# Causal attention of four heads in one query tile, values by query tile, and narrower rank comparisons, in an eight-stage graph model

## What is computed

```python
# x = x + _L1_ffn_ref(_layernorm(x), ...)
weights = (jnp.einsum('bsd,do->bso', x, wr) + br)[..., 0]
_, idx = jax.lax.top_k(weights, k)
sel_idx = idx[:, :kk]
h = jax.nn.gelu(jnp.einsum('bkd,dh->bkh', sel, w1) + b1)
y = jnp.einsum('bkh,hd->bkd', h, w2) + b2
y = y * w_sel[..., None]
processed = jnp.zeros_like(x).at[batch_idx, sel_idx].set(y)
return processed + x
...
# inside x = x + _L3_ffn_ref(x, ...)
q = q * cos + _rotate_half(q) * sin
k = k * cos + _rotate_half(k) * sin
scores = jnp.einsum('bhtd,bhsd->bhts', q, k) / jnp.sqrt(jnp.float32(HD))
scores = jnp.where(causal[None, None], scores, jnp.float32(-1e+30))
att = jax.nn.softmax(scores, axis=-1)
y = jnp.einsum('bhts,bhsd->bhtd', att, v).transpose(0, 2, 1, 3).reshape(Bx, Tx, Cx)
x = x + y @ wo.T
```

## Time and profile before

| | |
|---|---|
| median of 3 runs | 4642.03 us (4640.98 to 4642.9) |
| the profiled execution, by the same clock as the runs | 4647.35 us |
| its span, first to last instruction | 4645.3 us |
| mean granted clock of PE in it | 0.824 |
| busy in the span: PE, DVE, ACT, POOL | 76%, 61%, 44%, 37% |
| the mod stage | about 2465 to 2666 us of the span |
| the mha3 stage | about 3628 to 4212 us of the span |

### The profile page before, as it was taken

The page is one execution under the profiler, slowest core; times in us unless marked ns, Lnnn a source line. Parts: engine busy times, 40 slices in busy tenths (PEclk is TensorE's granted clock), DMA queues, the critical chain, the costliest instruction groups (busy, mean ns, idle before and its releaser), DMA issues. The chain is left out here.

```text
span 4645.3 us, 80348 instructions
## 1 busy us (share of the span) xinstructions
PE 3532.3 (76%) x23571; PEld 2150.4 (46%) x23571; DVE 2839.6 (61%) x10823; ACT 2067.0 (44%) x5218; POOL 1717.0 (37%) x2167
## 2 busy tenths in 40 slices
PE   3999995666666649999896776479847788874994
PEld 1333334444444423333364566357636555542663
DVE  5677756555555566777588967612277566653444
ACT  1777773322222217777632265334347444441221
POOL 3555520000000014343293137744446444344445
PEclk9999995555555559999998987689969998986997
DMA  4444429500000024433100022144342000002445
GB/s 128 125 135 130 126 63 390 231 0 0 0 0 0 0 80 124 122 110 115 50 0 2 9 86 73 48 132 145 118 144 83 1 10 16 14 19 75 130 130 164
DMA packets 235811, 386.80 MB, mean 83 GB/s; under 512 B 25344, under 2 KB 157568, under 8 KB 227136
## 3 DMA queue, kind: packets, MB, share of 16 engines
q1 hardware_dynamic: 217152, 345.83, 22.8%
q0 software_dynamic: 18432, 38.31, 2.4%
HBM read 210.70 MB, written 173.34 MB: 83 GB/s over the span
## 5 line engine op out<-in xcount | busy, mean ns | idle before, releaser
L1482 DVE CUSTOM_DVE_ANT_0 mha_seen<-mha_score,mha_mask 128x512 f32<-128x512 f32 x1024 | 682.7, 688 | 378.6 <-PE mha_score L1245 372.5
L1386 ACT ACTIVATE mha_prob<-mha_turned 128x512 f32<-128x512 f32 x1024 | 587.3, 602 | 305.8 <-PE mha_turned L1259 298.1
L1638 PE MATMUL lstm_gates<-lstm_h_part,lstm_w_part 128*128 128x16 f16 x4608 | 278.8, 179 | 327.9 <-DVE lstm_h_part L1853 324.5
L1245 PE MATMUL mha_score<-mha_k_rows,mha_q_rows 96*128 96x512 bf16 x1024 | 398.7, 391 | 59.4 <-DMA mha_k_rows<-split_rows 39.0
L3152 POOL DMA_INDIRECT expert_rows<-expert_y,expert_target x320 | 306.5, 958 | 367.6 <-DVE expert_y L3298 150.8
L1638 PEld LDWEIGHTS lstm_gates<-lstm_h_part,lstm_w_part 128*128 128x128 f16 x4608 | 217.2, 107 | 481.2 <-DVE lstm_h_part L1853 475.5
L1259 PE MATMUL mha_turned<-mha_q_rows,mha_k_rows 99*128 99x512 bf16 x1024 | 390.0, 382 | 7.9 <-ACT mha_turned L1370 6.4
L1585 POOL TENSOR_TENSOR core_mid<-lstm_hist,lstm_per_unit 128x128 f32 x64 | 29.3, 458 | 888.0 <-DVE lstm_hist L1854 888.0
L1725 ACT ACTIVATE lstm_act<-lstm_gates 128x48 f32<-128x48 f32 x512 | 107.5, 210 | 429.7 <-PE lstm_gates L1638 429.7
L1258 PE MATMUL mha_turned<-mha_maskT,core_ident_bf 128*128 128x512 bf16 x768 | 295.0, 384 | 0.5 <-ACT mha_prob L1386 0.3
L3190 PEld LDWEIGHTS expert_out_ps<-expert_w,expert_hid 128*128 128x128 f32 (+1 forms) x2240 | 262.4, 191 | 39.3 <-issue 37.1
(11 more groups left out here) (550 smaller groups left out, 8834.7 us busy)
## 6 DMA issues: line engine op xcount, KB each, us to landing
routed_rows<-lstm_blank SPq DMA_DIRECT2D x66, 1056.0 KB, 26.9
gat_adj_raw<-adj SPq DMA_DIRECT2D x32, 1024.0 KB, 5.5
mha_q_rows<-split_rows SPq DMA_DIRECT2D x64, 384.0 KB, 4.0
mha_k_rows<-split_rows SPq DMA_DIRECT2D x64, 384.0 KB, 4.9
expert_x<-routed_rows SPq DMA_DIRECT2D x80, 264.0 KB
expert_w<-weights SPq DMA_DIRECT2D x80, 256.0 KB
core_params<-adj SPq DMA_DIRECT2D x16, 1024.0 KB, 6.1
combine_pair<-expert_rows SPq DMA_DIRECT2D x32, 512.0 KB, 4.9
```

The source lines that it names most:

```text
L1245: pe.matmul(score[n % 2][:, :], rows[0][s][0:ROWS, h, t * P:(t + 1) * P], rows[1][s][0:ROWS, h, :], start=True, stop=True).then_inc(S["sco ...
L1386: act.activation(prob[:, n % RING, :], turned[n % 3][:, :], ACT.Exp, scale=-1.0).then_inc(S["prob_ready"], 1)
L1482: dve.tensor_tensor_reduce(seen[n % 2][:, :], score[n % 2][:, :], mask[1 - s][:, t, :], 1.0, 3e38, ALU.add, ALU.min, low[g][:, t, j:j + 1] ...
L1638: return pe.matmul(out, w[:, g * P:(g + 1) * P], h_part[:, part, :], start=False, stop=stop, skip_group_check=True)
```

## The change

In mod: the comparisons of tile t cover only the columns in which their mask isn't zero, 0 to (t+1)·128 and t·128 to 512; the bias `mb2` is cut into three bf16 parts at the stage's start (`cut_bias`, DVE) and added by a bf16 matmul of ones with 512 columns ahead of `out`; POOL adds `xn` and the old rows (`residual`, to `base`), and DVE's last step multiplies, adds and writes the rows at once.

In mha3: one query tile per graph with all heads; scores read rows 32j to 32j+31 of it and of `kT`; the value products are made per query tile, each once its four items are copied; projections go one to an item; POOL sends rows before it makes the scales; the memsets of the query tiles and the wait `landed` are gone.

```diff
-            at = {"rows": 0, "early": (2, 4), "values": 3, "back": 6, "ctx": 9, "out": 11, "v": 12}
+            at = {"rows": 0, "early": (2, 3, 4, 5), "values": 3, "back": 7, "ctx": 10, "out": 12, "v": 13}
...
-                    if first:
-                        pool.wait_ge(S["zeros_set"], 8)
                     if b >= 4:
                         pool.wait_ge(S["r_scaled"], (b - 2) // 2)
-                    if b >= 6:
-                        router.landed(pool, (b - 6) // 2, b % 2)
-                    for j in range(4):
-                        rows = slice(32 * j, 32 * j + 32)
-                        pool.tensor_tensor(qT[s][j][rows, :], part[rows, 0, :], part[rows, 1, :], ALU.add)\
-                            .then_inc(S["rot_ready"], 1)
-                    pool.wait_ge(S["rot_ready"], 5 * b + 4 + 5)
+                    pool.tensor_tensor(qT[s][:, :], part[:, 0, :], part[:, 1, :], ALU.add).then_inc(S["rot_ready"], 1)
...
                     graph(b, b % 2, first=b == 0)
                 if b + 1 < B:
                     normalise(b + 1)
+                if b >= 5:
+                    half = (b - 5) % 2 * T
+                    router.scatter(pool, (b - 5) // 2, range(half, half + T))
                 if b % 2 and 0 <= (b - 3) // 2 < B // 2:
                     pool.wait_ge(S["tail"], (b - 1) * (2 * T + 3))
                     router.scales(pool, (b - 3) // 2)
-                if b >= 5:
-                    half = (b - 5) % 2 * T
-                    router.scatter(pool, (b - 5) // 2, range(half, half + T))
 
...
             def scores(b, s, n):
                 g, t, j = n // (4 * T), tile_of(n), n % 4
                 if n == 0 and rope:
-                    pe.wait_ge(S["rot_ready"], 5 * b + 5 + 5)
+                    pe.wait_ge(S["rot_ready"], 2 * b + 2 + 2)
                 elif n % (4 * T) == 0:
                     pe.wait_ge(S["qk_ready"], projections * b + 2 * g + 2 + 1)
                 pe.wait_ge(S["score_taken"], items * b + n + 1)
                 width = keys(t) * P
                 pair = s if rope else g
-                pe.matmul(score[n % 2][:, 0:width], qT[pair][j][:, t * P:(t + 1) * P], kT[pair][:, 0:width], start=True, stop=True)\
+                own = slice(32 * j, 32 * j + 32)
+                pe.matmul(score[n % 2][:, 0:width], qT[pair][own, t * P:(t + 1) * P], kT[pair][own, 0:width], start=True, stop=True)\
                     .then_inc(S["score_done"], 1)
...
-            def values(b, g, s):
-                done = b * (items // 2) + 2 * T * (g + 1) + 1
-                if g == 0:
+            def values(b, k, s):
+
+                t = ORDER[k]
+                own = slice(t * P, (t + 1) * P)
+                done = b * (items // 2) + 2 * (k + 1) + 1
+                if k == 0:
                     pe.wait_ge(S["v_ready"], b + 1 + 1)
-                pe.wait_ge(S["oT_ready"], groups * b + g + 1)
+                    pe.wait_ge(S["oT_ready"], b + 1)
                 pe.wait_ge(S["probT_act"], done)
                 pe.wait_ge(S["probT_dve"], done)
-                for u in range(T):
+                for u in range(keys(t)):
                     for j in range(4):
-                        first = u * P if rope else 0
-                        last = pe.matmul(o_ps[g][32 * j:32 * j + 32, first:], v32[s][:, u, 4 * g + j, :], probT[:, j, u, first:],
-                                         start=(u == 0), stop=(u == T - 1))
+                        last = pe.matmul(o_ps[0][32 * j:32 * j + 32, own], v32[s][:, u, j, :], probT[:, j, u, own],
+                                         start=(u == 0), stop=(u == t))
...
-                        values(b - 1, groups - 1, 1 - s)
-                    if n == at["values"] + 4 * T:
-                        values(b, 0, s)
+                        values(b - 1, T - 1, 1 - s)
+                    if n > 4 and n % 4 == at["values"]:
+                        values(b, n // 4 - 1, s)
...
             def copy_probT(b, n):
                 act.wait_ge(S["prob_free"], items * b + n + 1 + PR)
-                if n % (4 * T) == 0:
-                    act.wait_ge(S["pv_done"], groups * b + n // (4 * T) + 1)
+                if n % 4 == 0 and b:
+                    act.wait_ge(S["pv_done"], T * (b - 1) + n // 4 + 1 + 1)
...
-            rows_.normalise_all(pool)
+            pool.memset(bias_ones[:, :], 1.0).then_inc(S["bias_set"], 1)
...
+            def residual(b, s):
+
+                pool.wait_ge(S["xn_ready"], b + 1)
+                if not isinstance(b, int) or b >= 2:
+                    pool.wait_ge(S["x_taken"], b - 1)
+                apart(pool, core)
+                pool.tensor_tensor(base[s][:, :, :], rows_.xn[b % 3][:, :, :], core.x_res[:, b], ALU.add).then_inc(S["base_ready"], 1)
+
+            def graph(b, s, first=False, last=False):
+                rows_.normalise(pool, b)
+                residual(b, s)
...
+                if b >= 2:
+                    pe.wait_ge(S["x_taken"], b - 1)
+                pe.matmul(out_ps[s][:, :], bias_ones[:, :], flat(bias_rows[:, :, :]), start=True, stop=False)
                 pe.wait_ge(S["hid_free"], H * (b + 1) + 3)
-                pe.wait_ge(S["out_taken"], b + 1)
...
-            dve.wait_ge(S["tri_set"], 2)
-            dve.sem_inc(S["out_taken"], 2)
-            STEPS = T - 1 + WRITE_STEPS
+            STEPS = 2 * T
+
+            def cut_bias():
+
+                chain = Chain(dve, S["bias_chain"])
+                left = par("mb2")
+                chain.step(dve.memset(bias_rows[:, :, :], 0.0))
+                for i in range(3):
+                    chain.step(dve.tensor_copy(bias_cut[:, i, :], left))
+                    chain.settle()
+                    if i < 2:
+                        chain.step(dve.tensor_tensor(bias_left[:, :], left, bias_cut[:, i, :], ALU.subtract))
+                        chain.settle()
+                        left = bias_left[:, :]
+                for i in range(3):
+                    row = slice(32 * i, 32 * i + 1)
+                    chain.step(dve.tensor_copy(bias_rows[row, :, :], bias_cut[row, i, :].unsqueeze(1).broadcast_to([1, T, D])))
...
-                    for i, (tri, op) in enumerate(((earlier, ALU.is_ge), (later, ALU.is_gt))):
-                        chain.step(dve.scalar_tensor_tensor(hits[:, 2 * t + i, :], wrow[:, :], wcol[s][:, t:t + 1],
-                                                            tri[:, t, :], op, ALU.mult, accum_out=count[:, i, t:t + 1]))
+                    for i, (tri, op, lo, hi) in enumerate(((earlier, ALU.is_ge, 0, (t + 1) * P), (later, ALU.is_gt, t * P, N))):
+                        chain.step(dve.scalar_tensor_tensor(hits[:, 2 * t + i, lo:hi], wrow[:, lo:hi], wcol[s][:, t:t + 1],
+                                                            tri[:, t, lo:hi], op, ALU.mult, accum_out=count[:, i, t:t + 1]))
...
-                dve.tensor_tensor(y[:, :, :], out_ps[s][:, :].rearrange("p (t d) -> p t d", t=T),
-                                  par("mb2").unsqueeze(1).broadcast_to([P, T, D]), ALU.add).then_inc(S["out_taken"], 1)
-                dve.wait_ge(S["out_taken"], b + 1 + 2)
+                dve.wait_ge(S["base_ready"], b + 1)
                 for t in range(T):
-                    ins = dve.scalar_tensor_tensor(y[:, t, :], y[:, t, :], coef[:, t:t + 1], rows_.xn[b % 3][:, t, :],
-                                                   ALU.mult, ALU.add)
-                    if t < T - 1:
-                        chain.step(ins)
-                ins.then_inc(S["xn_free"], 1)
+                    ins = dve.scalar_tensor_tensor(core.x_res[:, b, t, :], out_ps[s][:, t * D:(t + 1) * D], coef[:, t:t + 1],
+                                                   base[s][:, t, :], ALU.mult, ALU.add)
+                ins.then_inc(S["x_taken"], 1)
+                dve.sem_inc(S["xn_free"], 1)
+                dve.wait_ge(S["x_taken"], b + 1)
+                for t in range(T):
+                    chain.step(dve.bn_stats(six[:, t, :], core.x_res[:, b, t, :]))
                 chain.settle()
-                dve.wait_ge(S["xn_free"], b + 1 + 3)
-                write_x(dve, chain, core, b, y[:, :, :], core.x_res[:, b], six)
+                for t in range(T):
+                    chain.step(dve.bn_aggr(core.x_stat[:, b, t, :], six[:, t, :]))
+                chain.settle()
```

63 lines of the change are left out of this document (32 added, 31 removed).

## The result

The changed kernel takes 4838.06 us (median of 4 runs, 4818.14 to 4846.53) against 4642.47 us; the ratio is 1.041, interval 1.039 to 1.043. The prediction said 4631, and 4675 at most. The profiled execution took 4818.14 us, its span 4816.3, with a mean granted clock of 0.786 instead of 0.824.

What follows compares the result with a forecast made beforehand. DVE was taken to bound mod, PE mha3. Terms -25 (mod), -3, +34, -2 and -15 (mha3) sum to -11 from the profiled 4647.35 us: 4636.3 as profiled, 4631 as median; range 4590 to 4675.

Steps and rivals of the forecast that it cites:

- part 5: mha3 scores on 32-row tiles: shape switches cost 0.22 us an item, 3.4 a graph, +34 us in all, bounds 0 and 77.
- rival D: mha3: 32-row scores hold PE's granted clock down, some 0.88 to 0.80 in twelve graphs, 35 us more, 4666; chance 0.07.
- The sign that the prediction named for D: mha3: a lower granted clock in plain graphs would show that scores filling 32 rows hold the clock down.
- Mod (-25): Mod stage: DVE's work falls under PE's, period 11.37 to 9.60 us; -25 us with the ends, bounds -28 and -12.
- where I had 3: Mod's start: `cut_bias` stands before PE's first `hid`, about 4 us, of which 3 lie past where `hid` began.
- The rival of a period of 10.5: Mod keeps a DVE or POOL chain: period 10.5, mod -12, total 4644, the same as before; chance 0.13.
- mha3, start (-3): Start of mha3: PE's 2.84 us wait for POOL's sums before its first score goes, -3 us.
- The price of a change of shape at one clock: mha3 scores: 0.08 us into the small tile and 0.14 out, 0.22 per item, 16 items, taken as 3.4 a graph.
- Values per tile (0, bounds of 5): mha3 value products by query tile and projections one per item: gains and waits set off, 0 us, bounds ±5.
- The end (-2): End of mha3: the last block of value products is shorter, at the lower clock, -2 us.
- POOL's order (-15): mha3: first of two sendings moves into the even graph, 2.5 us a pair, six pairs, -15 us; bounds 0 and -50.

## Why the prediction was wrong, point by point

**The step that failed** is part 5, tiles of 32 rows, by the road that rival D named and mis-sized. The prediction priced the new tiles by starts at the full clock, +34 us, and let the clock stay; the graphs became 176 us longer. Rival D let it go from 0.88 to 0.80, worth 35 us, with a chance of 0.07. It went to 0.61 in the routing graphs, 0.64 over the sixteen. All sixteen graphs took 523.9 us before and 699.8 after: +176 of the stage's +185; its start lost 2.5 us and its end gained 11. Two errors stand in D. Its slope was too small: PE busy grew in the even graphs from 27.3 to 44.7 us, since half the speed doubles the time of what runs at it, and the 6 us without work that PE had in a routing graph were used up first. And it had scores with few rows act as waits do, alone; the runs show that 65 rows alone cost 0.15 to 0.3%, the shape changes alone their own time, and both together 3.3 to 4.4%. Nor would the attention with adjacency have warned: from 300 to 400 us PE is busy in 96.6 us at a clock of 1.00, with matmuls of 96 and 99 rows and changes to tiles of 128*32 between them, in bf16. The sign that the prediction named for D, a lower clock in plain graphs, did show: 0.80 in b=1, though not in b=2.

**Mod (-25):** -26 in the two traces, -25 as timed alone. The mechanism was right, PE became the bound. The period is 9.39, not 9.60, so 15 periods save 30 us and not 27; the start costs more: PE's first `hid` waits for `cut_bias`.

```profile
2482.83 1.12 PE L2156 MATMUL mod_wrow<-core_ident,mod_wide 128*128 128x128 f32 x4 [1.49 <-DVE mod_wide L2320]
2486.84 5.38 PE L1928 MATMUL mod_hid_ps<-mod_xT,core_params 128*128 128x512 f32 x6 [2.90 <-DVEq L2313]
```

It begins at 2486.84, 5.3 us later than before, in a stage that began 1.5 later: 3.8 where I had 3. The rival of a period of 10.5 didn't happen.

**mha3, start (-3):** the wait for POOL ahead of the first score fell from 2.84 us to 0.19.

```profile
3630.20 1.16 PE L496 MATMUL mha_misc<-core_params 128*128 128x128 f32 x8 [0.78 <-DVE core_params L766]
3631.55 0.91 PE L520 MATMUL mha_score<-mha_kT,mha_qT 32*128 32x384 f32 x2 [0.19 <-POOL mha_kT L424]
```

**The price of a change of shape at one clock (0.22 an item, 3.4 a graph)** came out near: 28.2 against 25.4 for the plain graph of the changed kernel, 28.5 against 25.5 with 64 rows. Of the first, PE's busy time grew by 4.4 (23.44 to 27.87) and its waits shrank by 1.6, which I had let stand. The Trainium skill's rule that a change of tiling mode drains TensorE ("TensorEngine Tiling (Array Packing)", Key Properties) agrees with the trace as a cost: 0.19 us an item with 64 rows, 0.34 at the place shown above, two changes each, on both sides of the 0.16 a change that I had read a full drain to be.

**Values per tile (0, bounds of 5):** the kernel with all but the 32 rows and the order (4541) is 2 to 5 us slower than mod alone (4536 and 4539) on chips of one kind, inside the bounds; at the lower clock they cost more, as told. **The end (-2)** went the other way: from the last graph to the stage's end 59 us instead of 48, 11 longer, by POOL's order, which costs 10 us as timed alone.

**POOL's order (-15):** on a chip with remote waits the pair gained 4.8 us, nearly twice my 2.5, odd graphs 31.6 (I said 33 to 35), even 34.9 (up to 37). I had not looked at the places behind the last graph, where the same edit puts the scales behind a sending that waits: +10 to +12. On a chip without remote waits only this loss is left. In the changed kernel itself, bound by PE at 1.2 GHz, no gain can be seen, but the loss can: ACT waits 26.7 us for the scales.

```profile
ACT mha_r_rows L2494 <- POOL mha_r_scale L2466: 26.7, 1, 26.7
```

It waited 8.5 before.

**What is settled and what is open.** Shown: the line with the 32 rows makes the loss; rows have a dose; rows and changes of shape act together on the granted clock, on one chip. Open: what in the changes of shape counts; whether the values that are multiplied matter, since the 65-row kernels work on other scores; and why two executions on different chips differ in where the fall sets in (the plain graph b=2 stood at 1.00 in the first trace of the changed kernel and at 0.67 in the second). Why the remote waits occur was not looked into.

## What to carry to other kernels

A matmul that uses fewer rows was no faster here (0.41 us to the next start against 0.22), and with it the whole stage became much slower: zero rows that keep the full tile were worth 220 us here. Before a small tile is written between full ones, compare the granted clock over the whole stage, not the duration of one matmul or the clock of one graph; price such an edit at either clock. When a queue's order is changed for the steady state, write out its last rounds too: there the same order may put the late work behind a wait.
